# The attention's values' product for four heads at a time: groups, buffers and the places of the side work

## The reference

```
xn = ln(x, g_norm)
q = (xn @ Wq).reshape(b, n, HEADS, DIM_HEAD).transpose(0, 2, 1, 3)
kv = xn @ Wkv
k, v = (kv[..., :DIM_HEAD], kv[..., DIM_HEAD:])
...
q = l2norm(q) * q_scale
k = l2norm(k) * k_scale
sim = jnp.einsum('bhid,bjd->bhij', q, k) * SCALE
...
attn = jax.nn.softmax(sim, axis=-1)
out = jnp.einsum('bhij,bjd->bhid', attn, v)
out = out.transpose(0, 2, 1, 3).reshape(b, n, HEADS * DIM_HEAD)
return ln(out @ Wout, g_out)
```

## Time and profile before

| | |
|---|---|
| median of 3 runs | 2487.56 us (2485.59 to 2491.07) |
| the profiled execution | 2490.37 us, of which its span 2488.6 us |
| PE busy | 2344.3 us (94%) |
| DVE, ACT, POOL busy | 1739.9 (70%), 1237.4 (50%), 1337.5 us (54%) |
| mean granted TensorE clock | 0.983 |

### The profile page before, as it was taken

One profiled execution on the slowest core, in us unless ns is written; L12 is line 12 of the kernel. 1 busy time (PEld: TensorE's weight loads), 2 busy tenths in 40 slices (PEclk: granted clock), 3 DMA queues, 4 the chain that ended last, 5 costly groups with the idle time before them and its releaser, 6 DMA issues. The chain is left out here.

```text
span 2488.6 us, 56588 instructions
## 1 busy us (share of the span) xinstructions
PE 2344.3 (94%) x20593; PEld 1818.2 (73%) x20593; DVE 1739.9 (70%) x4089; ACT 1237.4 (50%) x3133; POOL 1337.5 (54%) x1464
## 2 busy tenths in 40 slices
PE   5899999999999999889999999989899999999998
PEld 3677777777777777557777777757687877877876
DVE  4586777777777877578888887347674665755763
ACT  2676766666676766445555553124333333333332
POOL 3586777778786868266666666016332332322322
PEclk8999999999999999999999999999999999999999
DMA  4001210001010100011222212153111212111112
GB/s 147 18 27 30 64 40 28 27 28 34 22 36 27 29 23 23 22 23 40 49 57 58 57 38 57 39 163 94 39 60 44 73 56 60 55 58 60 60 35 61
DMA packets 192530, 122.10 MB, mean 49 GB/s; under 512 B 87728, under 2 KB 170672, under 8 KB 192256
## 3 DMA queue, kind: packets, MB, share of 16 engines
q1 hardware_dynamic: 166768, 79.74, 11.7%
q10 hardware_dynamic: 25488, 38.73, 5.2%
HBM read 97.29 MB, written 21.14 MB: 48 GB/s over the span
## 5 line engine op out<-in xcount | busy, mean ns | idle before, releaser
L1615 POOL TENSOR_TENSOR m_hid_part<-m_hid,m_hid_part 128x512 fp32r<-128x512 f32 x176 | 238.1, 1353 | 553.8 <-ACT m_hid_part L1524 550.5
L991 POOL TENSOR_TENSOR a_bm<-a_bias,a_mask_add 128x512 f32<-128x512 f32 (+3 forms) x512 | 438.2, 877 | 119.9 <-DVE a_nm L726 113.9
L902 ACT ACTIVATE a_S<-a_S,a_nm 128x512 f32<-128x512 f32 (+3 forms) x512 | 289.6, 566 | 231.6 <-DVE a_nm L726 226.9
L726 DVE CUSTOM_DVE_ANT_0 a_S<-a_S,a_bm,a_nsn 128x512 f32<-128x512 f32 (+3 forms) x512 | 276.4, 546 | 78.2 <-PE a_S L476 69.3
L1536 ACT ACTIVATE m_hid<-m_G 128x512 f32<-128x512 f32 x176 | 105.5, 599 | 390.1 <-PE m_G L1470 355.8
L476 PE MATMUL a_S<-a_kT,a_qT 128*128 128x384 f32 (+3 forms) x1024 | 284.6, 361 | 0.7 <-DVE a_nm L726 0.5
L1697 DVE TENSOR_TENSOR m_hid<-m_hid,m_U 128x512 f32<-128x512 f32 x176 | 121.1, 688 | 223.2 <-PE m_U L1470 189.6
L1487 PE MATMUL m_Y<-m_hid_part,m_down_high 128*128 128x512 f32 x704 | 256.5, 405 | 12.3 <-POOL m_hid_part L1615 11.5
L1470 PE MATMUL m_G<-m_in,m_gate_high 128*128 128x512 f32 x704 | 251.8, 398 | 0.9 <-POOL m_up_low L1609 0.9
L1470 PE MATMUL m_U<-m_in,m_up_high 128*128 128x512 f32 x704 | 250.7, 396 | 1.5 <-DVE m_hid L1697 1.2
L486 PE MATMUL a_T<-s_ident,a_S 128*128 128x128 f32 x1280 | 230.2, 278 | 19.4 <-ACT a_PT L911 15.4
(11 more groups left out here) (326 smaller groups left out, 5263.2 us busy)
## 6 DMA issues: line engine op xcount, KB each, us to landing
a_o<-s_weight_rows SPq DMA_DIRECT2D x128, 128.0 KB, 3.0
m_spread<-s_w ACTq DMA_DIRECT2D x64, 256.0 KB, 3.3
m_spread<-s_w ACTq DMA_DIRECT2D x128, 128.0 KB, 2.9
a_x<-in_x SPq DMA_DIRECT2D x32, 128.0 KB, 2.8
s_hT<-a_hT SPq DMA_DIRECT2D x32, 128.0 KB, 2.2
d_x<-in_x SPq DMA_DIRECT2D x8, 512.0 KB, 5.3
d_h<-s_hT SPq DMA_DIRECT2D x8, 512.0 KB, 5.6
s_xg<-d_xg SPq DMA_DIRECT2D x8, 512.0 KB, 3.1
```

The source lines that it names most:

```text
L726: dve.tensor_tensor_reduce(S[:, n % S_SLOTS, 0:w], SB[n % 2][:, 0:w], bm[:, n % BM_SLOTS, 0:w], -1.0, nsn[:, tile % 2, h:h + 1], ALU.add, ...
L902: act.activation(S[:, n % S_SLOTS, 0:w], S[:, n % S_SLOTS, 0:w], ACT.Exp, scale=-1.0, bias=nm[:, tile % 2, h:h + 1], accum_out=den[:, tile ...
L991: pool.tensor_tensor(bm[:, n % BM_SLOTS, 0:w], bias[:, h, L - w:L], mask_add[b % 2][:, 0:w], ALU.add).then_inc(s["bm_ready"], 1)
L1615: pool.tensor_tensor(hid_part[1][:, q % H_SLOTS], hid[:, q % G_SLOTS], hid_part[0][:, q % H_SLOTS].bitcast(F32), ALU.subtract).then_inc(hi ...
```

## The change

The values' product is issued for four heads at a time in place of two, when step n - 3 is the last head of a group of four (before: n - 4, the second head of a pair); `pv_done` counts groups of four. There are five buffers PT in place of four, and two buffers hT in place of four. DVE copies the turned probabilities of four heads a tile (3, 4, 13, 14) in place of three (5, 13, 15). SLOTS and LATER move the side work of every engine, and FILLS moves `kv`, `qT1` and `pnT` to the other bank. The number of matmuls is the same. The diff, cut to its core:

```diff
-    QK_LAG, PV_LAG, S_SLOTS, PT_SLOTS = 2, 4, 5, 4
+    QK_LAG, PV_LAG, S_SLOTS, PT_SLOTS = 2, 3, 5, 5
+    PV_HEADS, HT_SLOTS = 4, 2
...
-        SLOTS = {"stat": -28, "xn": -21, "xT": -17, "q0": -16, "q1": -16, "kv": -14, "ss": -13, "qn": -11, "kT": -8,
-                 "null": -10, "qs0": -9, "qs1": -8, "qT0": -7, "qT1": -4, "qT2": -3, "qT3": -3, "diff0": 7, "weigh0":
+        SLOTS = {"stat": -26, "xn": -18, "xT": -17, "q0": -16, "q1": -15, "kv": -14, "ss": -13, "qn": -11, "kT": -8,
+                 "null": -5, "qs0": -9, "qs1": -7, "qT0": -7, "qT1": -4, "qT2": -3, "qT3": -3, "diff0": 9, "weigh0": 8,
...
-        DVE_HEADS = {5, 13, 15}
+        DVE_HEADS = {3, 4, 13, 14}
...
-                        if 0 <= n < NH * NT and n % 2 == 1:
-                            tile, h = divmod(n - 1, NH)
-                            wait_evac(pe, n - 1)
-                            wait_evac(pe, n)
+                        if 0 <= n < NH * NT and n % PV_HEADS == PV_HEADS - 1:
+                            first = n - PV_HEADS + 1
+                            tile, h = divmod(first, NH)
+                            for m in range(first, n + 1):
+                                wait_evac(pe, m)
...
-                                dve.wait_ge(s["pv_done"], (n - PT_SLOTS) // 2 + 1)
+                                dve.wait_ge(s["pv_done"], (n - PT_SLOTS) // PV_HEADS + 1)
```

More of the change, by code:

```diff
@@ L218, in attention_phase @@
         oT = sb("oT", [P, QT, P])
-        hT = sb("hT", [P, TT, KD, P])
+        hT = sb("hT", [P, HT_SLOTS, KD, P])
         nm = sb("nm", [P, 2, NH])
@@ L274, in attention_phase @@
         weight_in = [sem(f"weight{i}_in") for i in range(2)]
-        SLOTS = {"stat": -28, "xn": -21, "xT": -17, "q0": -16, "q1": -16, "kv": -14, "ss": -13, "qn": -11, "kT": -8,
-                 "null": -10, "qs0": -9, "qs1": -8, "qT0": -7, "qT1": -4, "qT2": -3, "qT3": -3, "diff0": 7, "weigh0":
[L279 to L283, removed]
+        SLOTS = {"stat": -26, "xn": -18, "xT": -17, "q0": -16, "q1": -15, "kv": -14, "ss": -13, "qn": -11, "kT": -8,
+                 "null": -5, "qs0": -9, "qs1": -7, "qT0": -7, "qT1": -4, "qT2": -3, "qT3": -3, "diff0": 9, "weigh0": 8,
+                 "wT0": 11, "diff1": 16, "scale0": 16, "weigh1": 19, "pnT": 19, "scale1": 24, "outp": 25, "ostat": 25,
+                 "hn": 28, "hT": 31}
+        LATER = {"PE": {}, "DVE": {"qT2": 2, "scale1": -1, "weigh1": -1, "diff1": 1, "weigh0": 1, "hn": -2, "null": 2,
+                 "diff0": -2, "scale0": 1, "qT0": -1, "ss": 1}, "ACT": {"qT3": 1, "diff1": 1, "xT": -1, "hT": 1, "qT1":
+                 -1, "diff0": -1}, "POOL": {"qs0": -2, "stat": 1, "ss": 2, "ostat": -2, "qs1": -1}, "SP": {}}
         BACK = ("diff0", "weigh0", "wT0", "diff1", "scale0", "weigh1", "pnT", "scale1", "outp", "ostat", "hn", "hT")
@@ L498, in _ @@
                                 pe.wait_ge(s["o_scaled"], 2 * tile)
[L499 to L504, removed]
+                            for m in range(first, n + 1, 2):
+                                at = m % 8 // 2 * P
+                                for j in range(tile % TT + 1):
+                                    for e in range(2):
+                                        last = pe.matmul(OB[h // 8][e * DH:(e + 1) * DH, at:at + P],
+                                                         v[tile // TT % 2][:, j],
+                                                         PT[:, (m + e) % PT_SLOTS, j * P:(j + 1) * P],
+                                                         start=j == 0, stop=j == tile % TT, skip_group_check=True)
                             last.then_inc(s["pv_done"], 1)
@@ L642, in scale @@
                     dve.wait_ge(weight_in[i], 32 * (t + 1))
[L643 removed]
+                    dve.wait_ge(s["pv_done"], NH // PV_HEADS * t + 8 // PV_HEADS * (i + 1))
                     if t > 0:
@@ L959, in _ @@
                         f = filled(name, t)
-                        if t >= TT:
-                            act.wait_ge(hT_out[t % TT], 16 * (t // TT))
+                        if t >= HT_SLOTS:
+                            act.wait_ge(hT_out[(t - HT_SLOTS) % TT], 16 * ((t - HT_SLOTS) // TT + 1))
                         for k in range(KD):
-                            last = act.activation(hT[:, t % TT, k], f[:, k * P:(k + 1) * P], ACT.Copy,
+                            last = act.activation(hT[:, t % HT_SLOTS, k], f[:, k * P:(k + 1) * P], ACT.Copy,
                                                   scale=go[:, k:k + 1])
```

6 lines of the change are left out of this document (3 added, 3 removed).

## The result

The changed kernel takes **2509.93 us** (median of 5 runs, 2505.56 to 2510.97), the kernel before 2487.56 (2485.59 to 2491.07 in 5 runs): a ratio of 1.0081, 95% interval 1.0069 to 1.0093. It is 22 us slower. 2461 us were predicted, 2436 to 2484.

What follows compares the result with a forecast made beforehand. TensorE was taken to bound the attention's steps (busy 904.17 of 954.00 us). The terms 43.5 - 5.5 - 10.5 - 1 = 26.5 us less gave a median of 2461 us, with eight in ten from 2436 to 2484.

Steps and rivals of the forecast that it cites:

- Half the groups: Values' product on TensorE: 128 fewer groups, each saving 0.20 us entering and 0.14 leaving, 43.5 us less; bounds 17.5 to 43.5.
- Rival B: Values' product on TensorE: only the idle time in the rows returns, 10 us net, 2477 us; chance 0.15.
- The group one step behind its last copy: Behind step 5, TensorE is 0.5 us short against DVE's copy; it would wait for scores anyway, so nothing added.
- Rival C: Copies' queue on ACT delays three groups a tile: slower, 115 us at worst, deciding above 0.21 us a group; chance 0.11.
- banks, hT and copies: Moved banks, fewer hT buffers and 32 extra copies on DVE (15.5 us, covered by removed waits): all priced at zero.
- The work between steps 3 and 8: In 24 tiles of widths 2 to 4, DVE shortens 0.44 us less than TensorE: 10.5 us lost, bounds 0 to 21.
- Clock: Dips of the granted clock cost 1.2 us, once a batch; eight again, none or sixteen being 10 us either way.
- Tail: Last tile's weights are turned behind four heads, before the round trip through DRAM: 1 us later, bounds 0.5 and 2.
- Width 1: Tiles of width 1, where TensorE isn't the bound: half of 11 us saving lost, 5.5 us, bounds 0 and 11.

Runs made afterwards that it cites:

- the sums alone: Groups of four, four steps behind, six PT buffers (2486.68 us), with the norms' sum one step earlier on DVE and POOL: 2506.26 us, 1.0072.
- the copy first: The changed kernel, three steps behind, with DVE's copy of head n - 2 ahead of its scores' operation on head n: 2506.00 us, 1.0086.
- the late inputs: Pairs, four steps behind, new places (2519.97 us), with x's norm and the norms' sum put back to their earlier places: 2513.81 us, 1.0100.

## Why the prediction was wrong

*Half the groups*, 43.5 us: **right in kind, too large in size**. Four steps behind, where no group waits for a copy, fours against pairs measured 33.3 us, and 21 at equal buffers. The 44.5 us three steps behind agree with the forecast by luck: only 16 us of them are busy time, the rest is that half as many groups come too late. The group of 24 holds the unit from 625.83 to 627.29, the 1.46 us that were forecast, in this timeline of the changed kernel:

```profile
625.83 1.29 PEld L505 LDWEIGHTS a_O<-a_PT,a_v 128*64 128x64 f32 x24 [0.17 <-issue]
627.29 0.30 PEld L477 LDWEIGHTS a_S<-a_kT,a_qT 128*128 128x128 f32 x2 [0.17 <-issue]
```

Rival B, that only the idle time in the rows comes back, is out as the whole story: TensorE's busy time fell by 34 us as well. By the Trainium skill (TensorEngine Tiling (Array Packing), Key Properties) a change of mode drains the array. The trace can't show a drain; the prediction's estimate of 14 us, from the depth that the Trainium skill gives for a drain, is less than the 21 to 33 that the runs showed.

*The group one step behind its last copy*, "isn't added twice", priced at nothing: **this step failed**. Three steps in place of four cost 34.5 us at pairs and 23.2 at fours, some 11 of the latter by the step alone. Two things were wrong in it. First, its count of DVE's work behind the turning of head 3, 1.18 us, starts with the scores of step 5; in the row DVE is still at the sum a_ss, 1.28 + 0.18 us, so that the copy ends 2.04 us after the turning began (614.08 to 616.12). The sum stood behind step 3 before and stands behind step 4 now (LATER has it one step more on DVE). Second, the reason given, that TensorE would wait for the scores anyway: behind the late group stands the next scores' product, so the 0.99 us reaches DVE, which waits (69.3 to 157.1 us over the phase), and then TensorE waits for DVE and ACT again. Rival C had the mechanism and the right sign, and gave the point from which it decides, 0.21 us a group. The loads in front of the product stand idle for 55.2 us (40.9 + 14.3) against 17.7 (16.7 + 1.0) with four steps and six buffers, 0.29 us a group more, so it passed that point; of these 37 us 23 show in the time. Its place was mostly wrong: it looked at the three groups whose last head ACT copies, and 33 of the 55 us stand in front of the fourth, whose last head is DVE's. By its price in the sum above it would not have made the kernel slower alone: with the places at nothing it is -33 + 23 = -10.

*The other moved places*, not priced at all, with banks, hT and copies "All zero": **this failed as well, and by more**. The sum has no term for the places of the sums, the statistics, the weighing and the output, and they cost 32 us at pairs, all of it idle time of TensorE. I looked for each edit's own cover, and found it each time; the parts put back one at a time say that the edits can't be priced one by one, and no single row of the trace of before shows that.

*The work between steps 3 and 8*, 0.44 us a tile short, 10.5 us: no run measures it by itself. DVE's wait for a_rr did go, as forecast; the sum a_ss that now stands a step later in the stretch wasn't counted. Taking the sum out again (the sums alone, above) didn't help fours, but that was four steps behind, where the group doesn't wait for the copy; at three steps it is untested.

*Clock*, ten either way: inside its bounds. There are 11 stretches with the lower level in the phase where there were 8, and in windows of 1 us the clock falls short of full by 31 us in sum in place of 21, 10 us more; the 1.2 us of the earlier trace rows are what one row lost. How much of the 10 us reached the time isn't shown, but with the copy first the sum is 22 and the kernel as slow. The mean of the execution is 0.979 against 0.983.

*Tail*, 1 us: it can't be told from nothing. From the attention's steps to the next phase it is 14 us in both kernels (1011 to 1025 and 1033 to 1047), and the round trip through DRAM again sets the end (DVE waits 4.72 us for it, 5.86 in the earlier trace rows).

*Width 1*, 5.5 us lost: not measured by itself. In the batch of the earlier trace rows the tiles of width 1 to 4 became longer by 0.99, 0.69, 0.42 and 0.87 us.

What stays open: which passages carry the some 27 of the 32 us of the places that the late inputs don't explain; the parts of the tables put back one at a time don't show it. Of the 23 us of the step, the share of the buffers is known to some 6 us only. Whether the edits to fours lose by their waits or by the lower clock isn't shown, nor why fours at the old places take 128 us more.

## What to carry to other kernels

A saving that is read from rows as a cost per group (here 0.34 us, 43.5 us in all) came back in kind, as 21 to 33 us where nothing else changed; it is the terms put at zero that must be tested. When a batch is made larger and its distance to the last producer shorter in one change, price the distance as a wait of the in-order engine and of whoever waits for what is queued behind it, and count what already stands in the producer's queue at that moment. A table of places that was fitted to one order of work is a term of its own: here it was as large as the saving, and with the distance kept at four steps the fours only just paid for it (0.9998). No version measured beat the kernel before.

## What the runs showed of the hardware that was not expected

- Going from loads of 128*128 to loads of 128*64 and back costs 0.34 us a group by the earlier trace rows (0.20 entering, 0.14 leaving), in 32 bit floats. Groups of 24 and of 32 loads agree with the leaving half: 1.46 us above, and 1.90 us from 555.42 to 557.32 in the changed kernel, are 0.055 us a load and 0.14. The tables of waits show only the entering half, in pieces of at most 0.2 us by "issue": 35.1 us with 256 groups, 16.7 with 128.
- More idle time of TensorE went with a lower granted clock in several kernels, though not in all. At fours and old places, three steps behind, the slowest kernel measured, it is 0.94 in the attention's steps, against 0.98 for the same places with pairs, four steps behind the earlier trace rows:

```profile
56.00:1135.00 1079.00, 926.59 (x6726) 750.49 (x6727) 686.63 (x2065) 644.01 (x1994) 714.80 (x761) 0.94 0.09 27
```

TensorE is busy there for 22 us more than in the earlier trace rows with 128 groups fewer, and in windows of 1 us the clock falls short of full by 68 us in sum in place of 21: a loss of this kind shows as busy time, where nobody looks for a wait. The counterexample is the banks put back at pairs: TensorE is idle for some 97 of 1011 us there, against 50 of 954 in the kernel before, at the same clock of 0.98.
